# First group of a fused recommender tower in two parts: 16 samples at a time through gather, store, reload, pair products and x1, and W1 split in four pieces

## The chip, the cores and the metric

The kernel runs on one core of one Trainium2 chip. The metric is the device time of one execution in microseconds, taken as the median of several runs. Engines are named as in the profile: PE (matrix multiply), PEld (its weight loads), DVE (VectorE), ACT (ScalarE), POOL (GpSimd, which also issues the gathers and the folding transfers) and SP (SyncE, which issues the other transfers).

## The reference

There are 512 samples. For each, 39 rows of 16 numbers are gathered from 39 tables. Three interaction layers follow, each a sum over pairs of a raw field j and a field k of the layer before; then the three layers' sums over the 16 numbers and 16 dense features pass through a small three-layer network.

```
e  = stack([tbl_f[ids[:, f]] for f in 0..38])            # 512 x 39 x 16
x1 = einsum('hjk,bjd,bkd->bhd', W0, e, e)  + b0          # 128 fields
x2 = einsum('hjk,bjd,bkd->bhd', W1, e, x1) + b1
x3 = einsum('hjk,bjd,bkd->bhd', W2, e, x2) + b2
z  = concat([x1.sum(d), x2.sum(d), x3.sum(d)]);  h = concat([z, dense_ctx])
y  = relu(relu(h @ W_top1 + b) @ W_top2 + b) @ W_top3    # 512 x 1
```

## The kernel before

**Tiling.** A column is one (sample, d) pair, 8192 in all. A group is 512 columns (32 samples), a tile 128 columns; there are 16 groups of 4 tiles. Buffers exist twice, one half for even groups and one for odd.

**Getting a group's rows (x0).** POOL adds table starts to the ids (L317) and issues 10 indirect gathers for a group (L324), each for one row of 16 numbers on 125 partitions. SP stores them to a scratch tensor in device memory (L245) and loads them back turned (L255), so that a field is a partition and the group's 512 columns lie along it, in copies one below the other (for groups 0 and 1 all four pieces from memory, later one from memory and three copied inside SBUF, L259). SP then makes the shifted copies from which pairs are formed: three transfers for the first factor (L268), one for each second factor (L273). Second factors 1 to 6 share three slots, so number 4, 5 and 6 wait until earlier pairs are formed. After its last shifted copy SP goes on to the store and the reload of the next group.

**x1.** DVE forms seven blocks of pairs (L653, 117 x 512 each, two buffers); PE multiplies each by W0 folded over symmetric pairs (L394, full fp32) into one bank; ACT adds the bias (L542) and rounds the result to a high part x1_hi (L551); DVE computes the rest x1_lo (L660).

**x2.** For each of a group's 4 tiles PE does 10 chunks of 4 fields j (the last has 3): x1_hi times W1_hi, x1_hi times W1_lo, x1_lo times W1_hi (L426 to L428), into five banks in rotation. ACT takes six chunks of a tile and multiplies each unit by the column's x0 value (L567); DVE takes the other four and adds onto ACT's (L671). POOL then issues a transfer that adds one half of the tile's products onto the other half (L346, 'fold'), and DVE adds up the rest (L703, four steps), the first of which waits for that transfer. The x2 of tile t is summed beside tile t + 2. A third product with a diagonal matrix that POOL builds (L334) gathers sums over d for layer 3 (L411 on PE, L556 on ACT), one tile later still. Layer 3 and the small network come after the last group.

**Order of the work.** Every engine's program is written out by hand. Inside a group the position p = 10 * tile + chunk (0 to 39) is the clock: `FORM_AT` says after which chunk DVE forms a block of pairs for the next group (6, 10, ... 30), `PAIR_AT` where PE multiplies it (11, 15, ... 35), position 8 is where PE transposes the next group's x0 (L402), ACT takes bias and x1_hi of the next group behind chunk 35 (`BIAS_AT`), DVE x1_lo at 36, and the sums of DVE (`SUM_AT`) come at chunks 1, 3, 5 and 7 of a tile. So the first sum of tile 0 is at position 21.

**The start.** SP loads ids, table starts, the two halves of W0, W1 (2.4 MB), then eleven small constants. POOL issues the 10 gathers of group 0, the 10 of group 1 and, once the constants are there, 9 of the 10 of group 2 (`GATHERS_EARLY`), one behind the other (L350 to L358); only then comes its work of group 0, where in its second tile it issues the fold of tile 0:

```
if fold_before:
    scaled(t - 1)
diagonal(t, s, first)
if fold_before:
    fold((s - 1) % TILES_PER_GROUP)
```

ACT rounds W1 whole (L592), DVE takes the rest whole (L728), PE runs matmuls with no use (`warm_up`, L448) around the first transposes and the seven pair products, and starts group 0 when x1_lo is there.

Of the kernel before, what the change touches and what calls it, by code (L numbers as in the profile page):

```python
# [25 lines left out]
P = 128  # L26
COLS = 512
# [39 lines left out]
PIECES = [(0, 3), (3, 4)]  # L67
TOP1, TOP2 = 512, 256
# [5 lines left out]
AHEAD = 2  # L74
GATHERS_EARLY = 9
# [3 lines left out]
BIAS_AT = 5  # L79
# [6 lines left out]
def tower_program(nc, ids, starts, table, dense_t, pair_a, pair_b, w1, w2, b0, b1, b2,  # L86
# [6 lines left out]
    with ctx:  # L93
# [12 lines left out]
        idx = sb("idx", [ROW_PARTS, 2, GATHERS], i32)  # L106
        emb = sb("emb", [ROW_PARTS, 2, GATHERS * D])
# [56 lines left out]
        g_psum = small_bank[:, 0:TB * J1].rearrange("p (j b) -> p j b", b=TB)  # L164
        x0t_psum = x0t_bank[:, 0:TILES_PER_GROUP * F].rearrange("p (s f) -> p s f", f=F)


        ids_loaded = sem("ids_loaded")
        w_loaded = sem("w_loaded")
# [43 lines left out]

        def scaled_before(t, c):
# [9 lines left out]
        def _(sp):  # L224
            sp.dma_start(ids_all[:, :], ids).then_inc(ids_loaded, 16)
            sp.dma_start(table_at[:, :], starts).then_inc(ids_loaded, 16)
            sp.dma_start(pair_a_raw, pair_a).then_inc(w_loaded, 16)
            sp.dma_start(pair_b_raw, pair_b).then_inc(w_loaded, 16)
            sp.dma_start(w1_raw, w1).then_inc(w_loaded, 16)
            for slot in range(TILES_PER_GROUP):  # L230
# [11 lines left out]
            def store_rows(g, half):  # L242

                sp.wait_ge(gathered[half], (g + 2 - half) * (8 * GATHERS))
                sp.dma_start(emb_dram[bass.ds(g * ROW_PARTS, ROW_PARTS), :], emb[:, half, :]).then_inc(emb_stored, 16)  # L245

            def load_x0(g, half, at_once):


                sp.wait_ge(emb_stored, (g + 1) * 16)  # L250
# [10 lines left out]
            def factors(g, half):  # L261

                if not (isinstance(g, int) and g == 0):
                    sp.wait_ge(pair_ready, g * BLOCKS)
# [17 lines left out]
            x0_of(0, 0, at_once=True)  # L282
            factors(0, 0)
# [25 lines left out]
        def _(pool):  # L309
            pool.memset(x0t[:, :, :], 1.0).then_inc(ones_set, 1)  # L310
            pool.wait_ge(ids_loaded, 16 * 2)

            def index(g, half):

                if not (isinstance(g, int) and g < 2):
                    pool.wait_ge(gathered[half], (g - half) * (8 * GATHERS))
                pool.tensor_tensor(idx[:, half, :], ids_all[:, bass.ds(g * GATHERS, GATHERS)], table_at[:, :],  # L317
                                   ALU.add).then_inc(index_ready, 1)
                pool.wait_ge(index_ready, g + 1)
                if not (isinstance(g, int) and g < 2):  # L320
                    pool.wait_ge(emb_stored, (g - 1) * 16)
# [66 lines left out]
        def _(pe):  # L388
            def pair_product(g, b):

                pe.wait_ge(pair_ready, g * BLOCKS + (b + 1))
                if b == 0 and not (isinstance(g, int) and g == 0):
# [4 lines left out]
            def transpose_x0(half, first):  # L397

                if first:
                    pe.wait_ge(x0_loaded, 16 * X0_LOADS)  # L400
                for s in range(TILES_PER_GROUP):
                    mm = pe.transpose(x0t_psum[:, s, :], rep[0:F, half, s * P:(s + 1) * P], ident[:, :])  # L402
                mm.then_inc(x0t_mm, 1)
# [26 lines left out]
            def group(g, half, first=False, last=False):  # L430
                for s in range(TILES_PER_GROUP):
                    t = g * TILES_PER_GROUP + s
                    pe.wait_ge(x1_lo_ready, g * len(PIECES) + (1 if s < 3 else 2))
                    for c in range(CHUNKS):
                        p = s * CHUNKS + c
                        t_chunk(t, s, c, first and s == 0, g + 1 if p == X0T_AT and not last else None)
                        if c == G_AT and not (first and s <= BEHIND):
                            g_product(t - BEHIND - 1, (s - BEHIND - 1) % TILES_PER_GROUP)
                        if not last:
                            if p == X0T_AT:  # L440
                                transpose_x0(1 - half, False)
                            if p in PAIR_AT:
                                pair_product(g + 1, PAIR_AT.index(p))
# [10 lines left out]
            transpose_x0(0, True)  # L454
            warm_up(WARM_UP[1])
            for b in range(BLOCKS):
                pair_product(0, b)
# [367 lines left out]
```

## Time and profile before

| | us |
|---|---|
| median of 3 runs | 673.19 (672.38 to 675.87) |
| the profiled execution's own time | 672.67 |
| its span, first to last instruction | 670.6 |
| first matmul of group 0 | 44.37 |
| first matmul of group 1 | 79.71 |

```profile
POOL 6878766575656565755666675656575221121000
PEclk9799999999999999999999999999999999999999
```

The lines cut the span into 40 equal slices of 16.8 us; a digit is the busy share in tenths (for PEclk the share of full speed that TensorE's clock was granted). Line numbers L.. are those of the kernel before. Gathers and folding transfers stand with POOL as the time that it takes to issue them; they land later.

### The profile page before, as it was taken

The page shows a single profiled execution, that of the slowest core. Times are in us where ns is not written, and L with a number is a line of the kernel's source. Part 1 is how long each engine was busy: PE and PEld are TensorE (multiplying, and loading weights), DVE is VectorE, ACT ScalarE, POOL GpSimd, SP SyncE. Part 2 cuts the span into 40 slices and gives each one's busy share as a digit, 9 for nine tenths or more (in the row PEclk, how much of TensorE's full clock was granted, in tenths as well). Part 3 has the DMA queues.
Part 4 walks back from the last instruction along what each step waited for, and adds up shares of the span by engine and source line. Part 5 has one row for each costly group of instructions (what it writes and reads, how often), then busy time and mean ns, then how long its engine had stood idle before and what let it go on. Part 6 is the DMA issues. An engine that isn't in the chain of part 4 may idle for free.

```text
span 670.6 us, 11899 instructions
## 1 busy us (share of the span) xinstructions
PE 641.9 (96%) x2516; PEld 461.4 (69%) x2516; DVE 521.2 (78%) x1478; ACT 488.3 (73%) x1692; POOL 361.1 (54%) x308
## 2 busy tenths in 40 slices
PE   0689999999999999999999999999999999999998
PEld 0246777777777777777777777777777777785483
DVE  0346888878888888888888878888888888897590
ACT  1137877778787868787877878787868787897293
POOL 6878766575656565755666675656575221121000
PEclk9799999999999999999999999999999999999999
DMA  6457687767676777667667767676777657567100
GB/s 225 60 92 168 112 183 133 173 131 162 124 160 128 159 150 163 142 134 155 139 144 134 167 130 161 124 160 129 160 150 162 142 102 178 126 122 215 31 1 0
DMA packets 61944, 91.05 MB, mean 136 GB/s; under 512 B 34599, under 2 KB 38548, under 8 KB 61671
## 3 DMA queue, kind: packets, MB, share of 16 engines
q0 software_dynamic: 14192, 51.02, 42.0%
q1 hardware_dynamic: 47734, 39.85, 21.2%
q8 instruction: 6, 0.10, 0.1%
q14 instruction: 12, 0.09, 0.0%
HBM read 10.59 MB, written 1.28 MB: 18 GB/s over the span
## 4 chain that ended last, share of the span: by engine, by line
PE 91%; POOL 3%; DMA 3%; issue 2%; SPq 1%; ACT 0%; DVE 0%; ACTq 0%; POOLq 0%
PE t_bank L426 22%; PE t_bank L427 21%; PE t_bank L428 21%; PE x_bank L394 14%; PE small_bank L411 5%; POOL emb L324 3%; PE t_bank L491 1%; PE t_bank L471 1%; PE t_bank L502 1%; PE t_bank L503 1%; PE t_bank L514 1%; PE t_bank L505 1%; DMA emb<-in_table,idx 1%; PE x0t_bank L402 1%; DMA emb_scratch<-emb 1%
## 5 line engine op out<-in xcount | busy, mean ns | idle before, releaser
L567 ACT ACTIVATE prod<-t_bank,x0t 128x128 f32<-128x128 f32 x1472 | 417.5, 377 | 114.6 <-PE t_bank L428 109.3
L671 DVE SCALAR_TENSOR_TENSOR prod<-t_bank,x0t,prod 128x128 f32<-128x128 f32 x1024 | 287.9, 343 | 80.1 <-PE t_bank L428 75.8
L426 PE MATMUL t_bank<-w_hi,x_hi 128*128 128x512 f32 (+1 forms) x640 | 307.5, 480 | 0.6 <-DVE x_lo L660 0.3
L427 PE MATMUL t_bank<-w_lo,x_hi 128*128 128x512 f32 (+1 forms) x640 | 247.8, 387 | 0.0
L428 PE MATMUL t_bank<-w_hi,x_lo 128*128 128x512 f32 (+1 forms) x640 | 247.0, 386 | 0.0
L324 POOL DMA_INDIRECT emb<-in_table,idx x160 | 211.8, 1324 | 48.5 <-issue 46.8
L334 POOL TENSOR_TENSOR diag<-x0t,mask 128x320 f32<-128x320 f32 x64 | 87.8, 1372 | 195.4 <-DVE prod L671 97.7
L426 PEld LDWEIGHTS t_bank<-w_hi,x_hi 128*128 128x128 f32 x640 | 120.2, 188 | 54.7 <-issue 29.7
L427 PEld LDWEIGHTS t_bank<-w_lo,x_hi 128*128 128x128 f32 x640 | 120.5, 188 | 47.1 <-issue 25.3
L428 PEld LDWEIGHTS t_bank<-w_hi,x_lo 128*128 128x128 f32 x640 | 120.1, 188 | 24.2
L703 DVE TENSOR_TENSOR prod<-prod 128x768 f32<-128x768 f32 (+2 forms) x192 | 117.4, 611 | 6.0 <-DMA prod<-prod 5.7
L394 PE MATMUL x_bank<-pairs,w_pair 117*128 117x512 f32 x224 | 114.6, 594 | 2.7 <-DVE pairs L653 1.9
L653 DVE TENSOR_TENSOR pairs<-shared 117x512 f32<-117x512 f32 x96 | 65.5, 682 | 6.8 <-DMA shared<-rep 6.8
L346 POOL DMA_DIRECT2D prod<-prod x63 | 60.5, 961 | 0.0
L394 PEld LDWEIGHTS x_bank<-pairs,w_pair 117*128 117x128 f32 x224 | 41.8, 190 | 15.6 <-DVE pairs L653 6.3
L411 PE MATMUL small_bank<-diag,x 128*128 128x320 f32 x128 | 45.0, 433 | 0.0
L556 ACT ACTIVATE G<-small_bank 128x320 f32 (+1 forms) x64 | 29.1, 454 | 4.8 <-PE small_bank L411 4.8
L448 PE MATMUL t_bank<-w_pair 117*128 117x512 f32 x20 | 13.2, 816 | 16.3 <-DVE w_pair L726 16.3
L411 PEld LDWEIGHTS small_bank<-diag,x 128*128 128x128 f32 x128 | 23.9, 188 | 6.8 <-issue 0.8
L534 ACT ACTIVATE x0t<-x0t_bank 128x39 f32<-128x39 f32 x64 | 13.8, 221 | 10.7 <-PE x0t_bank L402 9.2
L542 ACT ACTIVATE x<-x_bank,bias 128x512 f32<-128x512 f32 x16 | 11.4, 715 | 13.2 <-PE x_bank L394 13.2
L625 ACT ACTIVATE w_hi<-G 128x512 fp32r<-128x512 f32 x20 | 12.6, 632 | 11.5 <-PE t_bank L505 10.5
(73 smaller groups left out, 242.8 us busy)
## 6 DMA issues: line engine op xcount, KB each, us to landing
prod<-prod POOLq DMA_DIRECT2D x63, 768.0 KB, 7.1
shared<-rep SPq DMA_DIRECT2D x96, 234.0 KB
shared<-rep SPq DMA_DIRECT2D x48, 78.0 KB
emb<-in_table,idx POOLq DMA_INDIRECT x160
G<-in_w SPq DMA_DIRECT2D x1, 2496.0 KB
rep<-rep SPq DMA_DIRECT2D x28, 78.0 KB
rep<-emb_scratch SPq DMA_DIRECT2D x20, 78.0 KB
prod<-in_w SPq DMA_DIRECT2D x1, 1536.0 KB, 7.1
```

Source lines behind the costliest of these rows:

```text
L324: pool.indirect_dma_start(out=emb[:, half, i * D:(i + 1) * D], out_offset=None, in_=table, in_offset=bass.IndirectOffsetOnAxis(ap=idx[:, h ...
L334: pool.tensor_tensor(diag[:, slot, :, :], x0t[:, slot, :].unsqueeze(2).to_broadcast([P, J1, TB]), mask[:, :].unsqueeze(1).to_broadcast([P, ...
L346: pool.dma_start(prod[:, slot, 0:HALF, :].rearrange("p j h -> p (j h)"), prod[:, slot, HALF:, :].rearrange("p j h -> p (j h)"), accum_op=A ...
L394: pe.matmul(x1_bank[:, :], w_pair[:, b * H:(b + 1) * H], pairs[:, b % 2, :], start=b == 0, stop=b == BLOCKS - 1).then_inc(pair_mm, 1)
L411: pe.matmul(small_bank[:, 0:TB * J1], x2[:, slot % 2, :], diag[:, slot, :, :].rearrange("p j b -> p (j b)"), start=True, stop=True).then_i ...
L426: pe.matmul(acc, hi, w1_hi[:, cols], start=True, stop=False)
L427: pe.matmul(acc, hi, w1_lo[:, cols], start=False, stop=False)
L428: pe.matmul(acc, lo, w1_hi[:, cols], start=False, stop=True).then_inc(t_mm, 1)
L567: last = act.activation(prod[:, s, SLOT[c] + u, :], t_bank[c % T_BANKS][:, u * H:(u + 1) * H], ACT.Copy, scale=x0t[:, s, j:j + 1])
L653: dve.tensor_tensor(pairs[:, b % 2, :], first, rep[0:PAIRS, half, :] if b == 0 else second[:, k, :], ALU.mult).then_inc(pair_ready, 1)
L671: last = dve.scalar_tensor_tensor(unit, t_bank[c % T_BANKS][:, u * H:(u + 1) * H], x0t[:, s, j:j + 1], unit, ALU.mult, ALU.add)
L703: dve.tensor_tensor(out, left, right, ALU.add).then_inc(summed, 1)
```

## The change

Group 0 is handled as two parts of 16 samples (256 columns, 2 tiles). A part has a gather of its own: two samples' halves folded on 126 (124) partitions, so 5 gathers a part in place of 10 for the group. It has its own ids (four small loads a part: part 0's ahead of the weights, part 1's and then the whole ids behind W1), its own store (2 transfers), reload (4), shifted copies (3 + 6) and semaphores. The six second factors of a part lie in space of `prod` that is free then, so they need no slot. Part 0's x1 is made before group 0 starts, in a bank of its own; part 1's is made inside group 0, with pairs at positions 7 to 13, products at 10 to 16, x1_hi ahead of chunk 17 and x1_lo at 18. What group 0 does for group 1 moves back: x0 transposes from position 8 to 22, pairs from 6, 10, ... 30 to 24, 26, ... 36, products from 11, 15, ... 35 to 26, 28, ... 38, bias and x1_hi from behind 35 to behind 39, x1_lo from 36 to 39. The later groups are as before. W1 is rounded and its rest taken in pieces of 10, 10, 10 and 9 fields. POOL's order behind the parts (group 1's gathers, 9 of group 2, then group 0's diagonals and folds) stays.

```diff
+PARTS = 2
+W1_PIECES = [(0, 10), (10, 20), (20, 30), (30, F)]
+PART_X0T_AT = 8
+PART_FORM_AT = [7 + b for b in range(BLOCKS)]
+PART_PAIR_AT = [10 + b for b in range(BLOCKS)]
+PART_X1_AT = (1, 7)
+PART_LO_AT = 18
+FIRST_Z0_AT = 21
+FIRST_X0T_AT = 22
+FIRST_FORM_AT = [24 + 2 * b for b in range(BLOCKS)]
+FIRST_PAIR_AT = [p + 2 for p in FIRST_FORM_AT]
+FIRST_X1_AT = (3, 9)
+FIRST_LO_AT = 39
 # SP
-            sp.dma_start(ids_all[:, :], ids).then_inc(ids_loaded, 16)
-            sp.dma_start(table_at[:, :], starts).then_inc(ids_loaded, 16)
+            load_part_ids(0)
             sp.dma_start(pair_a_raw, pair_a).then_inc(w_loaded, 16)
             sp.dma_start(pair_b_raw, pair_b).then_inc(w_loaded, 16)
             sp.dma_start(w1_raw, w1).then_inc(w_loaded, 16)
+            load_part_ids(1)
+            sp.dma_start(ids_all[:, :], ids).then_inc(ids_loaded, 16)
+            sp.dma_start(table_at[:, :], starts).then_inc(ids_loaded, 16)
...
-            x0_of(0, 0, at_once=True)
-            factors(0, 0)
+            for part in range(PARTS):
+                x0_of_part(part)
+                factors_of_part(part)
 # POOL
+            def gather_part(part):
+                n = FOLDS * PART_SIZE[part]
+                pool.wait_ge(part_ids_loaded[part], 16 * PART_IDS_LOADS)
+                pool.tensor_tensor(part_idx[0:n, part, :], part_ids[0:n, part, :], part_at[0:n, part, :],
+                                   ALU.add).then_inc(part_index_ready, 1)
+                pool.wait_ge(part_index_ready, part + 1)
+                for c in range(PART_GATHERS):
+                    pool.indirect_dma_start(
...
-            for g in range(AHEAD):
-                index(g, g)
-                for i in range(GATHERS):
-                    gather(i, g)
+            for part in range(PARTS):
+                gather_part(part)
+            pool.wait_ge(ids_loaded, 16 * 2)
+            index(1, 1)
+            for i in range(GATHERS):
+                gather(i, 1)
             pool.wait_ge(small_loaded, 16 * SMALL_LOADS)
 
             index(AHEAD, 0)
 # PE, in group 0
+                        if first and p in PART_PAIR_AT:
+                            last_part_pair_product(PART_PAIR_AT.index(p))
 # ACT
-            act.activation(w1_hi[:, :], w1_raw, ACT.Copy).then_inc(w_split_hi, 1)
+            for a, b in W1_PIECES:
+                act.activation(w1_hi[:, a * H:b * H], w1_raw[:, a * H:b * H], ACT.Copy).then_inc(w_split_hi, 1)
```

## Rows read from the trace of the kernel before

**Rows 1.** the page, engine shares and the chain that ended last

```profile
PE 641.9 (96%) x2516; PEld 461.4 (69%) x2516; DVE 521.2 (78%) x1478; ACT 488.3 (73%) x1692; POOL 361.1 (54%) x308
...
PE 91%; POOL 3%; DMA 3%; issue 2%; SPq 1%; ACT 0%; DVE 0%; ACTq 0%; POOLq 0%
```

**Rows 2.** busy time of engines by stretch; PEclk is the granted clock

```profile
21.80:27.90 6.10, 0.63 (x2) 0.01 (x1) 3.15 (x2) 0.00 (x0) 5.49 (x3) 0.87 0.51 51
28.40:32.10 3.70, 3.70 (x7) 1.57 (x6) 0.00 (x0) 0.49 (x4) 3.03 (x3) 0.50 0.42 95
...
79.70:115.60 35.90, 35.90 (x147) 26.73 (x146) 30.10 (x91) 28.36 (x105) 23.00 (x19) 1.00 0.72 148
115.60:151.60 36.00, 35.98 (x147) 26.74 (x146) 30.30 (x92) 28.47 (x105) 21.57 (x19) 1.00 0.71 149
```

**Rows 3.** timeline of the start: start us, us, engine, line, operation

```profile
3.99 1.43 POOL L324 DMA_INDIRECT emb<-in_table,idx  x1 [0.33 <-POOL idx L317]
...
11.75 0.43 SPq L238 DMA_DIRECT2D w<-in_top  x1
...
15.13 4.36 ACT L592 ACTIVATE w_hi<-G 128x4992 fp32r<-128x4992 f32 x1 [13.09 <-DMA G<-in_w]
...
19.52 5.36 DVE L728 TENSOR_TENSOR w_lo<-G,w_hi 128x4992 fp32r<-128x4992 f32 x1 [3.30 <-ACT w_hi L592]
...
19.64 6.35 POOL L324 DMA_INDIRECT emb<-in_table,idx  x1 [0.30 <-POOL idx L317]
...
20.65 0.30 SPq L245 DMA_DIRECT2D emb_scratch<-emb  x1
...
40.15 0.22 POOL L317 TENSOR_TENSOR idx<-ids_all,table_at 125x10 int32<-125x10 int32 x1
...
42.39 0.69 ACT L542 ACTIVATE x<-x_bank,bias 128x512 f32<-128x512 f32 x1 [13.24 <-PE x_bank L394]
...
44.37 0.47 PE L426 MATMUL t_bank<-w_hi,x_hi 128*128 128x512 f32 x1 [0.30 <-DVE x_lo L660]
```

**Rows 4.** groups by line, POOL, 4 to 19 us

```profile
L324 POOL DMA_INDIRECT emb<-in_table,idx x10 | 12.4, 1236 | 3.1 <-issue 2.7 <-POOL idx L317 0.3
```

**Rows 5.** timeline of POOL, group 0: the fold of tile 0

```profile
57.58 0.99 POOL L346 DMA_DIRECT2D prod<-prod  x1
```

**Rows 6.** timeline of DVE in groups 0 and 1

```profile
62.04 0.68 DVE L653 TENSOR_TENSOR pairs<-shared 117x512 f32<-117x512 f32 x1
64.48 0.96 DVE L703 TENSOR_TENSOR prod<-prod 128x768 f32<-128x768 f32 x1 [1.77 <-DMA prod<-prod]
65.36 1.12 DVE L671 SCALAR_TENSOR_TENSOR prod<-t_bank,x0t,prod 128x128 f32<-128x128 f32 x4
...
87.66 0.69 DVE L653 TENSOR_TENSOR pairs<-shared,rep 117x512 f32<-117x512 f32 x1 [0.58 <-DMA shared<-rep]
```

**Rows 7.** issues by line: KB each, median us to landing

```profile
shared<-in_top SPq DMA_DIRECT2D x1, 768.0 KB, 5.1
...
shared<-in_top SPq DMA_DIRECT2D x1, 32.0 KB, 5.0
```

**Rows 8.** the chain in order of time: one pair product

```profile
65.08 0.86 PE x_bank L394 x2
```

**Rows 9.** timeline of PE around the start of group 1

```profile
79.71 0.51 PE L426 MATMUL t_bank<-w_hi,x_hi 128*128 128x512 f32 x1
...
89.03 1.02 PE L394 MATMUL x_bank<-pairs,w_pair 117*128 117x512 f32 x2
```

**Rows 10.** timeline of SP, groups 2 and 3

```profile
63.85 0.32 SPq L245 DMA_DIRECT2D emb_scratch<-emb  x1
...
81.06 2.37 SPq L268 DMA_DIRECT2D shared<-rep  x3
```

**Rows 11.** timeline of SP, one group later

```profile
99.61 0.32 SPq L245 DMA_DIRECT2D emb_scratch<-emb  x1
...
114.37 2.38 SPq L268 DMA_DIRECT2D shared<-rep  x3
```

More of the change, by code:

```diff
@@ L224, in _, with load_part_ids @@
         def _(sp):
-            sp.dma_start(ids_all[:, :], ids).then_inc(ids_loaded, 16)
-            sp.dma_start(table_at[:, :], starts).then_inc(ids_loaded, 16)
+            def load_part_ids(part):
+                begin, n = PART_BEGIN[part], PART_SIZE[part]
+                for to, src in ((part_ids, ids), (part_at, starts)):
+                    for fold in range(FOLDS):
+                        sp.dma_start(to[fold * n:(fold + 1) * n, part, :],
+                                     src[begin:begin + n, fold:fold + PART_IDS]).then_inc(part_ids_loaded[part], 16)
+            load_part_ids(0)
             sp.dma_start(pair_a_raw, pair_a).then_inc(w_loaded, 16)
@@ L391, in pair_product @@
                 pe.wait_ge(pair_ready, g * BLOCKS + (b + 1))
-                if b == 0 and not (isinstance(g, int) and g == 0):
+                if b == 0:
                     pe.wait_ge(x1_ready, g)
@@ L395, in pair_product, with part_pair_product, last_part_pair_product, transpose_x0 @@
                           start=b == 0, stop=b == BLOCKS - 1).then_inc(pair_mm, 1)
[L397 to L401, printed above, removed]
+            def part_pair_product(b):
+                pe.wait_ge(early_pair_ready, b + 1)
+                pe.matmul(part_x1, w_pair[:, b * H:(b + 1) * H], pairs[:, b % 2, part_cols(0)],
+                          start=b == 0, stop=b == BLOCKS - 1).then_inc(early_pair_mm, 1)
+            def last_part_pair_product(b):
+                pe.wait_ge(pair_ready, b + 1)
+                pe.matmul(x1_bank[:, part_cols(1)], w_pair[:, b * H:(b + 1) * H], pairs[:, b % 2, part_cols(1)],
+                          start=b == 0, stop=b == BLOCKS - 1).then_inc(pair_mm, 1)
+            def transpose_x0(half, tiles=range(TILES_PER_GROUP), done=x0t_mm):
+                for s in tiles:
                     mm = pe.transpose(x0t_psum[:, s, :], rep[0:F, half, s * P:(s + 1) * P], ident[:, :])
-                mm.then_inc(x0t_mm, 1)
+                mm.then_inc(done, 1)
             def g_product(t, slot):
@@ L524, in _, with copy_x0t @@
         def _(act):
-            def copy_x0t(g, s, first):
+            def copy_x0t(g, s, first=False):
                 t = g * TILES_PER_GROUP + s
-                act.wait_ge(x0t_mm, g + 1)
+                if first and s < PART_TILES:
+                    act.wait_ge(early_x0t_mm, 1)
+                else:
+                    act.wait_ge(x0t_mm, g + 1)
                 if not first:
@@ L571, in group @@
             def group(g, first=False, last=False):
+                x1_at = FIRST_X1_AT if first else X1_AT
                 for s in range(TILES_PER_GROUP):
```

221 lines of the change are left out of this document (169 added, 52 removed).

## The prediction

> **What bounds the kernel now.** I read the page first: PE is busy 96% of the span and holds 91% of the chain that ended last [rows 1]. The windows by stretch say whether that is real: in groups 1 and 2 PE is busy 35.90 of 35.90 and 35.98 of 36.00 us at a granted clock of 1.00, while DVE has 30.1 and ACT 28.4 [rows 2]. So a group costs 36 us of PE, nothing later gives back what a group loses, and what remains outside is the start: group 0's first matmul is at 44.37 us [rows 3], group 1's at 79.71 [rows 9]. The question is by how much the change moves group 1's start, and what group 1 finds late.
>
> The timeline of the start shows POOL as the engine in front: 29 gathers one behind the other, 10 of group 0, 10 of group 1 and 9 of group 2, each 1.24 us and some 0.3 apart [rows 4], so 1.51 us each. One is much longer: the gather that starts at 19.64, just behind the start of DVE's W1 rest (19.52, 5.36 us), takes 6.35 us and ends 1.1 us behind DVE's end [rows 3]. Only when all 29 are out does POOL reach group 0, and its fold of tile 0 is issued at 57.58 [rows 5]. DVE's first sum of tile 0 (position 21) starts at 64.48, having waited 1.77 us for that transfer: 6.9 us after the issue [rows 5, 6]. Today PE starts so late that this hardly shows. A group 0 that starts earlier runs into it.
>
> **Part by part.**
>
> *The start itself.* Part 0 needs 5 gathers. Its ids are four loads in place of two, so the first gather goes from 3.99 to some 4.7 and the five are in at 14. SP, though, has six more loads to issue before it comes to the store: its list ended at 11.75 + 0.43 [rows 3], 16 loads in 11.4 us, 0.7 each (small ones less); 6 more give 14.5 to 16.5, I take 15.5, where the store was at 20.65. From that store to the first matmul were 23.7 us; half-width pairs, no slot waits and half-width x1 take some 5 of it (estimate; 1 to 9). Group 0 then starts at about 34 (30 to 39), 10 us earlier. The W1 pieces end near 22.5 instead of 24.9; nothing waits for them, as x1 is later. They cost nothing: the ACT and DVE time is hidden beside the gathers.
>
> *What POOL does to it.* Gathers are 29 as before. Two things differ. Part 1's ids are issued behind W1, which landed at 15.13 [rows 3] and is pushed to about 15.9 by the loads ahead. Do small loads wait for a large one ahead of them on the same queue? In the end of the trace a 32 KB load issued right behind a 768 KB one took 5.0 us, the large one 5.1 [rows 7]: yes. So part 1's first gather is at about 16.9, where POOL could have gone on at 12.4: 4.5 us idle. (The Trainium skill, DMA: Bandwidth & Descriptors, section Queues, rings and completion order, says that SP's transfers use one ring per DMA engine and are taken from it in ring order; the trace agrees as far as the 5.0 us go. Without that rule the stall would be nothing.) And DVE's four W1 pieces, about 17.0 to 22.5, lie right beside part 1's five gathers. The one long gather stretched by 5.1 us; in pieces the same 5.4 us can hold up between 1 and 4.5 us, I take 2.2. (The Trainium skill, GPSIMD Engine Reference, section 8, Key points, has GpSimd sharing its SBUF interfaces with VectorE, with contention where a VectorE instruction has two SBUF inputs, which the W1 rest has; the row agrees. It gives no duration.) Part 1 ends at 16.9 + 5 x 1.51 + 2.2 = 26.6, the index work is 0.55, group 1's ten gathers with the first a little longer and 0.3 of holds 15.6: group 2's index at 42.7 where it was at 40.15 [rows 3]. From there POOL's order is unchanged, 17.4 us to the fold and 6.9 to its landing. So DVE's sum of tile 0 can start at F = 67.0, not at 64.48: +2.5. Bounds: no wait for ids and no holds give -4.0 (20 gathers at 1.51 and three index steps from 4.7), all holds +4.7.
>
> *Part 1 inside group 0.* Its rows come at about 28, store 30 to 35, reload to 40, copies to 50; its pairs (position 7 on) wait, its products are seven of half width, 0.43 us each (0.86 for the full pair of matmuls [rows 8]), 3 us of PE. PE passes position 20 near 57. Chunks may run five banks ahead, so PE stands at position 26 by 61. All this lies before 67.0, so it costs nothing now; without that cover it would be 3 us of PE and some 6 of waits.
>
> *From F to group 1.* Before, 79.71 - 64.48 = 15.2 us, with four products of the next group left. Now all seven are left, and the first cannot start before DVE has done, behind the wait, two sums (0.96 [rows 6] and about 0.5), chunks 22 and 24 (1.12 each [rows 6]) and the first block of pairs (0.68): 4.1 us with their overlaps. Then 7 products x 0.86 = 6.0 and positions 27 to 39. A position is (36.0 - 6.0) / 40 = 0.75 us of PE, its small products shared in [rows 2], so 13 x 0.75 = 9.8. Form and product stand two positions apart, where it was five; pairs take 0.68 and a chunk 1.12 of DVE in 2.4 us of PE, so DVE just keeps up, no charge. At the boundary bias and x1_hi now come behind ACT's last chunk: 1.1 us for its three scalings, and 1.98 from bias to first matmul, as in the start (42.39 to 44.37 [rows 3]). Sum 4.1 + 6.0 + 9.8 + 3.1 = 23.0, 7.8 more than before. Below, PE's head start of three positions could be better used (+5); above, late forms (+9).
>
> *The clock.* PE idles from about 61 to 71. After an idle stretch of 6 us (21.8 to 27.9, PE busy 0.63) the granted clock was 0.50, that is 1.2 GHz of 2.4, over the next 3.7 us [rows 2]. Half of that is lost where PE binds: +1.5 (0 to 2.2).
>
> *What group 1 finds late.* SP stores group 2 only after its last shifted copy of group 1, which waits for the fourth block of pairs. Before: that block at 62.04, store at 63.85 [rows 6, 10], group 2's first pairs at 87.66, after a wait of 0.58, so 23.8 us with nothing to spare. Now the fourth block is at position 30: F + 4.2 + two products + four positions + its own 0.6 and the slow clock, F + 11 = 78.0; store 79.8; first pairs at 103.6, or 101.2 at the pace of a group later, where the store to the first-factor copy took 14.8 us (99.61 to 114.37) and not 17.2 [rows 10, 11]. The product follows 1.4 us later [rows 6, 9], 102.6 to 105.0. PE would want it 9.3 us after group 1's start [rows 9], 91.5 + 9.3 = 100.8. So PE waits 1.8 to 4.2 us more; I take 2, since the new stretch has fewer folds beside it. From group 2 on the periods are as before: the same block is at 18 again, with 22 positions to the next form.
>
> *Sum.* +2.5 + 7.8 + 1.5 + 2.0 = +13.8 on the profiled execution's own 672.67 (span 670.6 and 2.1 around it): 686.5. The median of the runs is 0.5 above that execution, well inside the uncertainty. The ten microseconds won at the start all become waiting in front of tile 0's sum.
>
> **Rivals.** (1) *The fold binds, but little is added behind it.* The clock is not charged because DVE sets the pace there, group 2's rows come at the quick pace, PE's head start is used: +1 + 5 + 0 + 0 to 2, about 679.5. For it: terms of one stretch overlap, as DVE and PE are near equal there. Against: the first form stands behind DVE's wait, and the boundary chain is serial. (2) *POOL is early, no slower than before.* If part 1's ids land early and the pieces leave gaps between them, the fold is issued 4.0 us earlier (53.6), and beside a quieter queue it could land in the shortest time that any fold of this trace took, 3.9 us in place of 6.9: F = 57.5. With +7.8 group 1 starts at 80.5, less 1 to 3 where PE has stood only briefly and kept its clock and head start: 78 to 80.5, and the time is 671 to 673.5. It decides from F below 56.7 (79.71 - 23.0). Against it are the 5.0 us of the small load and 29 gathers at 1.51, which no piece shortens. (3) *The gain passes.* If the sum of tile 0 did not hold the others up (chunks 22 to 26 going on from the banks while the fold lands, and the fold out by 50), the kernel would keep 10.4 of the start, less 3.0 of products and 3.1 at the boundary: 668. Against: DVE's list is in order, the sum stands ahead of chunk 22, and POOL's 29 gathers alone fill 4.7 to 50. (4) *The copies for part 1 are still later than the fold:* it needs 17 us more than I have for them; then 690 and up.
>
> **How the numbers follow.** Forecast 686.5: 0.55 (its own range 681 to 692); rival 1: 0.24; rival 2: 0.08; rival 3: 0.08; rival 4: 0.05. A change under 0.5% (3.4 us) can hardly be told from none with these runs. Faster 0.10 (rival 3 and a piece of 2), same 0.08, slower 0.82. The range 674 to 692 takes in rival 1 and the bounds of the holds.
>
> **What would show it.** In the changed trace: first matmul of group 0 at 30 to 39; POOL idle from about 12.4 to 16.5 before part 1's index; the W1 rest in four pieces with stretched gathers beside it; fold of tile 0 issued near 60; DVE's first 128x768 sum with a wait of 5 to 12 us on that transfer, near 67; PE idle before that, then a granted clock near 0.5; about 3 us between the last chunk of group 0 and group 1's first matmul, which is at 88 to 93; a wait of PE for group 2's first pairs; and periods of 36 us from then on. I am wrong if the first sum starts before 57, if group 1's first matmul is before 79, or if later groups take less than 35.9.

## The result, and the profile after

| | before | after |
|---|---|---|
| median of the runs, us | 673.3 (4 runs) | 699.45 (4 runs, 695.48 to 702.86) |
| ratio, 95% interval | | 1.037 [1.0322, 1.0417] |
| own time of the profiled execution, us | 672.67 | 695.48 |
| span, us | 670.6 | 693.5 |
| first matmul of group 0, us | 44.37 | 39.95 |
| DVE's first sum of tile 0, us | 64.48 | 64.88 |
| first matmul of group 1, us | 79.71 | 90.28 |
| what is lost behind that, us | 0 | 12.3 |

The change makes the kernel 3.7% slower, more than the 2% of the forecast and outside its range. Of the 22.9 us by which the span grew (22.8 by own time), 10.6 are there when group 1 starts (90.28 - 79.71); the other 12.3 come later, where nothing had been forecast. The profiled execution is the shortest of the four runs after, so the median is 4.0 us above the sums made on it.

The page first. Its instruction queue (q14) carried 12 packets before and carries 40 now, and of the chain that ended last 75% is PE, 8% DVE and 6% 'issue', where PE had 91% and 'issue' 2% [rows 1]. Before, then after:

```profile
q14 instruction: 12, 0.09, 0.0%
```

```profile
PE 650.8 (94%) x2530; PEld 464.9 (67%) x2530; DVE 521.9 (75%) x1489; ACT 490.5 (71%) x1697; POOL 346.5 (50%) x309
...
q14 instruction: 40, 0.33, 0.1%
...
PE 75%; DVE 8%; issue 6%; DMA 6%; SPq 3%; ACT 1%; DVEq 1%; POOL 0%; POOLq 0%; ACTq 0%
```

The windows by stretch come next, 36 us each from group 1's start (five of them; columns as in [rows 2]: length, sum busy of PE, PEld, DVE, ACT, POOL, then clock, DMA share, GB/s).

```profile
...
162.00:198.00 36.00, 35.46 (x143) 25.77 (x142) 29.39 (x88) 27.59 (x101) 21.02 (x19) 1.00 0.70 144
198.00:234.00 36.00, 35.98 (x148) 26.78 (x147) 30.28 (x92) 28.47 (x104) 23.13 (x20) 1.00 0.70 147
234.00:270.00 36.00, 34.61 (x141) 25.18 (x140) 29.52 (x88) 26.86 (x99) 19.84 (x19) 1.00 0.64 135
270.00:306.00 36.00, 35.98 (x149) 26.79 (x147) 30.30 (x91) 28.47 (x105) 21.60 (x20) 1.00 0.71 148
306.00:342.00 36.00, 34.53 (x140) 25.10 (x139) 28.84 (x86) 27.10 (x98) 19.79 (x18) 1.00 0.65 136
```

Every second group is whole (35.98 busy of 36, as all groups were before [rows 2]), and the ones between have 35.46, 34.61 and 34.53. The stretches slip as the kernel falls behind, so they show that there is a loss, not its exact size. The distance from each group's first matmul to the next group's gives the size: groups 3, 5, 7, 9, 11 and 13 take 37.1, 37.9, 38.0, 38.0, 38.9 and 37.8 us, all others from group 1 on 36.0 or less (before, every group takes 35.9 to 36.0). That is 11.7 us in six groups; the other 0.6 lies behind the start of the last group. The loss recurs once per pass of the loops: a pass holds two groups, and these six are the ones that begin a further pass. DVE's timeline at one of these places shows what it is (start us, us, engine, line, operation, idle before and what ended it):

```profile
234.97 0.29 DVE L878 TENSOR_TENSOR x<-prod 128x128 f32<-128x128 f32 x1
235.18 1.12 DVE L846 SCALAR_TENSOR_TENSOR prod<-t_bank,x0t,prod 128x128 f32<-128x128 f32 x4
240.06 0.96 DVE L878 TENSOR_TENSOR prod<-prod 128x768 f32<-128x768 f32 x1 [3.76 <-issue]
```

DVE ends its last chunk of group 4 at 236.3 and does nothing until 240.06, and the profile names no releaser: 'issue'. The sum at 240.06 is DVE's first work of group 5, the first that the third pass of the loop does behind the branch. Grouped over the loop:

```profile
L878 DVE TENSOR_TENSOR prod<-prod 128x768 f32<-128x768 f32 x171 | 106.0, 620 | 29.7 <-issue 22.9 <-DMA prod<-prod 6.7
```

22.9 us of 'issue' in 6 places, 3.8 each; PE loses 11.7 of them, about half. In the trace of before no sum waits for 'issue' in the loop (115 to 640 us); all that they wait for there is (us in total, times, longest):

```profile
DVE prod L703 <- DMA prod<-prod: 4.0, 5, 2.4
```

The start, SP first, then POOL, then DVE's first sum of tile 0:

```profile
4.46 6.50 SPq L278 DMA_DIRECT2D part_at<-in_starts  x2
11.01 2.35 SPq L286 DMA_DIRECT2D ids_all<-in_ids  x1
...
18.81 1.88 SPq L345 DMA_DIRECT2D emb_scratch<-part_emb  x2
24.55 1.83 SPq L351 DMA_DIRECT2D rep<-emb_scratch  x4
```

```profile
14.97 0.21 POOL L402 TENSOR_TENSOR part_idx<-part_ids,part_at 124x9 int32<-124x9 int32 x1 [4.42 <-DMA part_at<-in_starts]
15.49 2.50 POOL L406 DMA_INDIRECT part_emb<-in_table,part_idx  x1 [0.31 <-POOL part_idx L402]
18.30 2.48 POOL L406 DMA_INDIRECT part_emb<-in_table,part_idx  x1 [0.31 <-issue]
21.08 1.28 POOL L406 DMA_INDIRECT part_emb<-in_table,part_idx  x1 [0.30 <-issue]
...
41.13 0.22 POOL L415 TENSOR_TENSOR idx<-ids_all,table_at 125x10 int32<-125x10 int32 x1
...
58.38 1.00 POOL L444 DMA_DIRECT2D prod<-prod  x1
```

```profile
64.88 0.96 DVE L878 TENSOR_TENSOR prod<-prod 128x768 f32<-128x768 f32 x1 [5.40 <-DMA prod<-prod]
```

And the stretches of PE around the end of group 0 (columns as above):

```profile
60.00:64.40 4.40, 4.37 (x21) 3.04 (x19) 0.00 (x0) 3.72 (x15) 3.76 (x4) 1.00 0.99 184
64.40:69.00 4.60, 0.00 (x0) 0.00 (x0) 4.12 (x12) 0.47 (x2) 3.77 (x4) 0.92 0.93 222
69.00:72.00 3.00, 2.97 (x5) 1.75 (x6) 2.01 (x7) 0.00 (x0) 1.21 (x1) 0.50 0.96 193
72.00:75.00 3.00, 3.00 (x7) 1.75 (x6) 1.30 (x5) 1.14 (x4) 0.00 (x0) 0.50 0.47 123
...
77.00:87.30 10.30, 10.30 (x38) 6.77 (x36) 7.17 (x22) 5.98 (x24) 5.26 (x5) 1.00 0.71 139
87.30:90.30 3.00, 0.20 (x2) 0.03 (x1) 0.74 (x2) 1.99 (x5) 1.56 (x2) 1.00 0.21 57
```

PE does nothing from 64.4 to 69.0 and works at 0.50 of its clock (1.2 GHz) for the 6 us behind; then it stands idle from 87.3 to 90.3. The chain of waits shows the last stretch as single steps, one behind the other: ACT's last scalings, bias, x1_hi, DVE's x1_lo, PE.

```profile
58.38 6.48 DMA prod<-prod
...
87.78 0.62 ACT prod L706 x2
88.40 0.59 ACT x L681
89.01 0.53 ACT x_hi L690
89.56 0.57 DVE x_lo L835
90.28 0.49 PE t_bank L535
```

### The profile page after: what moved, and what is told of

Same layout as the page of the kernel before. It is cut to its first block, busy times and chain, and to the rows that moved or that the text cites. A ratio compares the mean times of both kernels' runs of the same rounds, so it can differ in the third digit from the quotient of the medians.

```text
span 693.5 us, 11966 instructions
## 1 busy us (share of the span) xinstructions
PE 650.8 (94%) x2530; PEld 464.9 (67%) x2530; DVE 521.9 (75%) x1489; ACT 490.5 (71%) x1697; POOL 346.5 (50%) x309
## 3 DMA queue, kind: packets, MB, share of 16 engines
HBM read 10.61 MB, written 1.28 MB: 17 GB/s over the span
## 4 chain that ended last, share of the span: by engine, by line
PE 75%; DVE 8%; issue 6%; DMA 6%; SPq 3%; ACT 1%; DVEq 1%; POOL 0%; POOLq 0%; ACTq 0%
PE t_bank L535 17%; PE t_bank L536 16%; PE t_bank L537 16%; PE x_bank L494 13%; DVE prod L846 5%; DMA prod<-prod 4%; PE small_bank L520 4%; DVE prod L878 2%; SPq L278 1%; PE t_bank L611 1%; PE t_bank L623 1%; PE t_bank L625 1%; PE t_bank L622 1%; PE t_bank L634 1%; DMA emb_scratch<-part_emb 1%
## 5 line engine op out<-in xcount | busy, mean ns | idle before, releaser
L535 PE MATMUL t_bank<-w_hi,x_hi 128*128 128x512 f32 (+1 forms) x640 | 311.2, 486 | 12.3 <-DVE prod L846 7.8
L422 POOL DMA_INDIRECT emb<-in_table,idx x150 | 190.5, 1270 | 45.4 <-issue 44.5
L432 POOL TENSOR_TENSOR diag<-x0t,mask 128x320 f32<-128x320 f32 x64 | 80.5, 1258 | 228.2 <-ACT prod L706 101.7
L878 DVE TENSOR_TENSOR prod<-prod 128x768 f32<-128x768 f32 (+2 forms) x192 | 118.6, 617 | 35.2 <-issue 22.9
L494 PE MATMUL x_bank<-pairs,w_pair 117*128 117x512 f32 x210 | 109.2, 601 | 4.7 <-DVE pairs L828 4.7
L828 DVE TENSOR_TENSOR pairs<-shared 117x512 f32<-117x512 f32 x90 | 61.3, 681 | 1.6 <-DMA shared<-rep 1.6
L494 PEld LDWEIGHTS x_bank<-pairs,w_pair 117*128 117x128 f32 x210 | 40.0, 192 | 12.8 <-DVE pairs L828 5.1
L567 PE MATMUL t_bank<-w_pair 117*128 117x512 f32 x20 | 14.6, 891 | 15.2 <-DVE w_pair L907 15.2
L775 ACT ACTIVATE w_hi<-G 128x512 fp32r<-128x512 f32 x20 | 12.6, 632 | 11.5 <-PE t_bank L625 10.5
L944 DVE TENSOR_TENSOR w_lo<-G,w_hi 128x512 fp32r<-128x512 f32 x20 | 13.7, 692 | 8.2 <-ACT w_hi L775 8.1
```

What stands on the lines that cost most here:

```text
L422: pool.indirect_dma_start(out=emb[:, half, i * D:(i + 1) * D], out_offset=None, in_=table, in_offset=bass.IndirectOffsetOnAxis(ap=idx[:, h ...
L432: pool.tensor_tensor(diag[:, slot, :, :], x0t[:, slot, :].unsqueeze(2).to_broadcast([P, J1, TB]), mask[:, :].unsqueeze(1).to_broadcast([P, ...
L494: pe.matmul(x1_bank[:, :], w_pair[:, b * H:(b + 1) * H], pairs[:, b % 2, :], start=b == 0, stop=b == BLOCKS - 1).then_inc(pair_mm, 1)
L535: pe.matmul(acc, hi, w1_hi[:, cols], start=True, stop=False)
L828: dve.tensor_tensor(pairs[:, b % 2, :], first, rep[0:PAIRS, half, :] if b == 0 else second[:, k, :], ALU.mult).then_inc(pair_ready, 1)
L878: dve.tensor_tensor(out, left, right, ALU.add).then_inc(summed, 1)
```

## The experiments

The theory after this reading had two halves: (a) in the start, what the forecast says, that POOL's order and the crowded end of group 0 eat the gain; (b) in the loop, that DVE fetches its program anew in every pass, because its loop now begins 16 instructions later. Counted in the built programs, DVE's loop is 308 instructions in both and begins at number 126 before and 142 after. The rival to (b) was that some transfer is late in every second group. Each time below is the median of its runs; the ratio is to runs of the kernel before on the same chip. The runs stem from several chips, on which the kernel before had medians of 672.9 to 675.7, so kernels of different chips are compared by ratio. Places within a kernel (a first matmul, a wait) are those of its one profiled execution. How far such places scatter can be seen from e2 and e10 below, whose start is that of the kernel before but for idle instructions: group 0's first matmul came at 46.04 and 45.65 where it was 44.37, group 1's at 80.62 and 80.79 where it was 79.71.

**e1: the changed kernel, DVE's loop moved 60 instructions on** (142 to 202), by waits that are already met, where DVE idles:

```diff
 # DVE, ahead of its first work
+            for _ in range(120):
+                dve.wait_ge(part_ids_loaded[0], 16 * PART_IDS_LOADS)
```

> The changed kernel with 120 waits that are already met (60 instructions) on DVE ahead of its first work, where it idles 14 us; nothing else. Theory (loop place): the changed kernel's two-group loop on DVE, 308 instructions long as before, begins 16 instructions later in DVE's program, no longer fits in what DVE holds of its program, and is fetched anew in each of its 7 passes; that is the 1.5 to 2.5 us that PE loses in every second group (12 of the 22.8 us). 60 instructions further on it fits again: some 12 us faster than the changed kernel (about 683 to 687), the waits of DVE's first sum for 'issue' gone, instruction-queue packets back from 40 to near 12. Rival (the gathers or transfers are late in every second group): the time stays at 695 to 700 and the waits stay.

Measured: 685.62 us, ratio 1.0156 [1.0098, 1.0214], where the changed kernel had 1.037 [1.0322, 1.0417]. Instruction queue and windows of the middle, which are whole again:

```profile
q14 instruction: 11, 0.08, 0.0%
```

```profile
223.70:259.70 36.00, 35.97 (x148) 26.76 (x147) 30.18 (x90) 28.37 (x103) 23.15 (x20) 1.00 0.70 146
259.70:295.70 36.00, 35.99 (x148) 26.78 (x147) 30.27 (x90) 28.36 (x103) 23.06 (x20) 1.00 0.70 146
...
```

So 60 instructions that do nothing make the kernel 2.1% faster, and the place of DVE's loop is the cause. Only DVE's loop was moved; those of the other engines begin where they do in the changed kernel. That the stall is a fetch is read from the packets and from the waits that name no releaser.

This profiled execution (687.17) is not free of loss behind group 1's start either. Group 1 starts 9.2 us later than in the kernel before, and 5.4 us more are lost after it: 1.6 in group 1, whose first 3 us (90 to 93) have a granted clock of 0.55 after PE's wait at the boundary; 2.5 in group 2, where DVE waits for group 3's first-factor copies; 1.3 behind the start of the last group.

```profile
88.92 0.49 PE L535 MATMUL t_bank<-w_hi,x_hi 128*128 128x512 f32 x1 [2.80 <-DVE x_lo L835]
```

```profile
137.49 0.69 DVE L828 TENSOR_TENSOR pairs<-shared,rep 117x512 f32<-117x512 f32 x1 [3.71 <-DMA shared<-rep]
```

The 1.6 us of group 1 recur in e5, e6, e7 and e9, the wait for copies does not.

**e2 and e10: the kernel before, DVE's loop moved 16 and 48 instructions on** (126 to 142 and 174), 32 and 96 met waits on `ids_loaded` in the same place.

> The kernel before with 32 met waits (16 instructions) on DVE ahead of its first work, so that its loop begins at the same instruction as the changed kernel's. Loop place: 10 to 14 us slower than before (683 to 687), PE windows of every second group at 33.5 to 35 us busy of 36, some 40 instruction-queue packets. Rival (something in the two parts disturbs the later groups): as before, 673.

Measured: 682.5 us, ratio 1.0121 [1.0078, 1.0165], 41 packets. A kernel that computes exactly what the one before does, with 16 idle instructions, loses 8 us, a little less than the 10 to 14 expected; by its trace groups 3, 5, ... 13 take 1.2 to 1.7 us more than the others, 8.9 in all.

> The kernel before with 96 met waits (48 instructions) on DVE ahead of its first work: DVE's loop begins at instruction 174 of its program, between the places that were slow (142) and fast again (202 to 204) and the fast one of before (126). If what counts is how many fixed blocks of the program the loop lies across (blocks of 256 by the Trainium skill, Runtime: NRT & Kernel Launch, section Instruction fetch mechanics), the edges seen so far put 174 still across three: as e2, 681 to 684, 38 to 42 packets of the instruction queue. Rival (16 instructions met one bad place only, for example one branch at an unlucky address): as before, 673, about 10 to 12 packets.

Measured: 679.8 us, ratio 1.0094 [1.0068, 1.012], 41 packets: slow, as the theory said, if by less (681 to 684 expected). DVE's waits in the loop, e2 and then e10 (who waited for whom: us in total, times, longest):

```profile
DVE prod L703 <- issue: 19.5, 6, 3.6
```

```profile
DVE prod L703 <- issue: 12.2, 6, 2.4
```

Both lose it in the same 6 passes, 3.3 and 2.0 us each. Places 126 and 129 (e11, e12) are fast, 142 and 174 slow, 202 and 204 fast. (The Trainium skill, Runtime: NRT & Kernel Launch, section Instruction fetch mechanics, says that an engine other than PE holds two blocks of 256 instructions, and that a taken branch whose target is in neither stalls until its block is fetched. An estimate from the figures in that section of the Trainium skill: a loop of 308 fits if it begins at most 204 behind the edge of a block, and the places seen agree if 63 to 75 instructions stand ahead of the built program, which no run here shows. The packets, 28 more over 7 passes of the loop, are 4 for each pass.)

**e3: the changed kernel, POOL's order.**

```diff
+FIRST_EARLY = 5
+FIRST_REST = [range(0), range(5, 10), range(0), range(0)]
+FIRST_NEXT = [range(0), range(0), range(0, 5), range(5, 9)]
...
-            for i in range(GATHERS_EARLY):
+            for i in range(FIRST_EARLY):
                 gather(i, 0)
...
+                    if first:
+                        for i in FIRST_REST[s]:
+                            gather(i, half)
+                        for i in FIRST_NEXT[s]:
+                            gather(i, 1 - half)
+                        continue
...
```

> The changed kernel with POOL's order in the start changed: 5 of group 2's gathers ahead of group 0's work in place of 9, the other 5 behind the fold of tile 0, and 5 and 4 of group 3's in tiles 2 and 3. Theory (POOL's order holds the fold of tile 0 up): the fold is issued at about 52 instead of 58.4, DVE's first sum starts at about 59 without a wait of 5.4, PE keeps its clock, and group 1's first matmul comes 7 to 10 us earlier than 90.3. Rival (the late pairs and the serial end of group 0 set it): under 3 us. The later groups stay as in the changed kernel, so the whole is 688 to 692 against 695 to 700.

Measured: 700.57 us, ratio 1.0383 [1.0335, 1.043]: nothing gained, where 688 to 692 were expected. The fold was issued at 55.67 (not 52; POOL had to wait for tile 0 to be scaled) and the first sum's wait fell from 5.4 to 1.5 us. But:

```profile
54.88 5.18 SPq L316 DMA_DIRECT2D rep<-emb_scratch  x4
64.02 2.41 SPq L328 DMA_DIRECT2D shared<-rep  x3
```

```profile
64.04 0.50 PE L544 MATMUL t_bank<-w_hi,x_hi 128*128 128x512 f32 x1 [2.21 <-DMA rep<-emb_scratch]
```

```profile
62.46 0.96 DVE L887 TENSOR_TENSOR prod<-prod 128x768 f32<-128x768 f32 x1 [1.54 <-DMA prod<-prod]
...
72.43 0.69 DVE L837 TENSOR_TENSOR pairs<-shared,rep 117x512 f32<-117x512 f32 x1 [2.84 <-DMA shared<-rep]
```

Group 1's reload, issued at 54.88, now runs beside the folding transfer and is not there before 64.0 (5.1 us from first issue to the shifted copies in the changed kernel, 9.1 here); PE waits 2.2 us for it, DVE 2.8 us for the first-factor copies, and group 1 starts at 91.44. My theory that POOL's order was the bound is true only up to the next one, less than 5 us behind, and removing the first pushed the second back.

**e4, e11, e12: parts of the change in the kernel before, without cutting the group.** e4 gives group 0's second factors 4 to 6 a place in `prod`, e12 splits W1 in four, e11 does both.

```diff
                 for b in range(1, BLOCKS):
+                    if isinstance(g, int) and g == 0 and b > SECOND_SLOTS:
+                        sp.dma_start(late_at(b), rep[b:b + PAIRS, half, :]).then_inc(late_second[b - 1 - SECOND_SLOTS], 16)
+                        continue
                     if b > SECOND_SLOTS:
                         sp.wait_ge(pair_ready, g * BLOCKS + (b + 1 - SECOND_SLOTS))
...
```

> The kernel before with one part of the change alone: in group 0 the second factors 4 to 6 go to free space of prod instead of waiting for a slot. Theory: the last pairs of group 0 are formed at about 37.5 to 38.5 instead of 40.48, the first matmul of group 0 is at 41.5 to 42.5 instead of 44.37, and since nothing of group 0 is held up by a fold at that shift (DVE waited 1.8 us with no loss of PE), the kernel is 1.5 to 3 us faster, 670.5 to 672. Rival (the fold of tile 0 at 64.5 takes the gain): 673, with a longer wait of the first sum.

Measured: e4 673.53 us over 10 runs, ratio 0.9977 [0.9949, 1.0004]. Group 0's first matmul came at 43.62 (41.5 to 42.5 expected), group 1's at 78.81, 0.8 and 0.9 us earlier than in the kernel before. DVE still waits for the last copies, and its last three blocks of pairs come at 37.56, 38.61 and 39.73, where 37.5 to 38.5 was expected for the last. The interval takes in 1, and 0.9 us is within the scatter of such places, so no gain is shown. (Its profiled execution is the slowest of its ten, 678.79, with its losses behind group 1's start.)

> The kernel before with W1 split in four pieces alone. Theory: nothing waits for the rest of W1 (x1 is later), so the same time within 1 us; the gather at 19.64 that took 6.35 us becomes two or three of 1.5 to 2.7 and group 1's rows are there 1 to 3 us earlier, hidden. Rival: those earlier rows shorten DVE's wait of 2.6 us for group 1's first pairs and give up to 1 us.

Measured: e12 674.84 us over 12 runs, ratio 1.0025 [1.0003, 1.0048]: a little slower, just clear of 1. Neither the theory (within 1 us) nor the rival (up to 1 us faster) fits. POOL and SP:

```profile
18.23 2.50 POOL L325 DMA_INDIRECT emb<-in_table,idx  x1 [0.30 <-issue]
```

```profile
22.28 0.30 SPq L246 DMA_DIRECT2D emb_scratch<-emb  x1
25.00 2.96 SPq L256 DMA_DIRECT2D rep<-emb_scratch  x4
```

Begun early, DVE's four pieces (15.4 to 20.9) fall on group 0's own last gathers (18.23: 2.50 us instead of 1.21), and group 1's gathers, no longer held, run beside group 0's store and reload: store at 22.28 where it was 20.65, reload 5.6 us long instead of 4.9, first matmul 47.44 instead of 44.37. Group 1 starts 1.9 us later. Of this, 1.3 to 1.7 and 0.9 to 1.1 us are no more than e2 and e10 show without any split. That in the kernel before the long W1 operation keeps POOL quiet just when group 0 needs the DMA engines is therefore the likely reading of these rows, not a shown cause.

> The kernel before with two parts of the change that do not cut the group: second factors 4 to 6 of group 0 in prod (as e4) and W1 split in four pieces. DVE's loop begins 3 instructions later than before; by e2 it went wrong at 16. Expected as e4, 0.5 to 2.5 us faster than before (671 to 673), the W1 pieces adding nothing but a shorter stretched gather; if 3 instructions are enough to push the loop out, 9 us slower.

Measured: e11 673.62 us over 12 runs, ratio 1.0 [0.9975, 1.0025], where 671 to 673 was expected. As far as these intervals can tell the two cancel; 3 instructions further on, the loop still fits (11 packets).

**e5, e6, e9: what else is in the end of group 0,** all on e1 (with its 60 idle instructions; e1 has a ratio of 1.0156 and group 1's start at 88.92). e5 moves group 0's work for group 1 forward, e6 lets DVE fold tile 0, e9 does both.

```diff
-FIRST_FORM_AT = [24 + 2 * b for b in range(BLOCKS)]
+FIRST_FORM_AT = [22 + 2 * b for b in range(BLOCKS)]
-FIRST_X1_AT = (3, 9)
-FIRST_LO_AT = 39
+FIRST_X1_AT = (3, 7)
+FIRST_LO_AT = 38
```

> The padded changed kernel (e1) with group 0's work for group 1 moved forward by two positions: forms at 22 to 34, products 24 to 36, bias and x1_hi ahead of ACT's chunk 38 (behind 37), x1_lo at 38. Theory (the end of group 0 is serial: 2.8 to 3 us between its last matmul and group 1's first): the gap shrinks to under 1 us and group 1 starts 2 to 3 us earlier than 88.9, the whole 2 to 3 us under e1. Rival (rows or the fold set it): the gap shrinks and the same time is waited at the first product; no gain.

Measured: 682.57 us, ratio 1.0129 [1.0083, 1.0176]. Group 1 starts at 86.22, 2.7 us earlier than in e1, as expected. Its wait at the boundary is 1.84 us instead of 2.80 (under 1 expected), and its first product waited 1.85 us instead of 4.22.

```diff
+                elif isinstance(t, int) and t == 0:
+                    dve.wait_ge(act_scaled, NA)
+                    dve.wait_ge(dve_scaled, ND)
+                    dve.tensor_tensor(prod[:, slot, 0:HALF, :], prod[:, slot, 0:HALF, :], prod[:, slot, HALF:, :],
+                                      ALU.add).then_inc(first_folded, 1)
...
```

> The padded changed kernel (e1) with the fold of tile 0 done by DVE itself (one more 128x1408 addition, some 1.5 us) and no folding transfer for that tile. Theory (the fold of tile 0 is what PE waits for): the 5.4 us wait of DVE goes, the first product of group 1 comes at 64 to 66 instead of 69.2, PE's clock stays at full, group 1 starts at 82 to 85 instead of 88.9 and the whole is 4 to 6 us faster than e1. Rival (group 1's rows are just behind the fold): DVE waits for the first-factor copies instead, product at 67 to 69, 0 to 2 us faster.

Measured: 681.15 us, ratio 1.0124 [1.0065, 1.0183]. The first product comes at 66.23, group 1 at 86.36. Between theory and rival: DVE's own addition in place of the folding transfer was worth 2.6 us of group 1's start, and PE's clock stayed at 1.00 up to there.

> e5 and e6 together (padded changed kernel; group 0's work for group 1 two positions earlier; tile 0 folded by DVE), the weights again from SP. If the two gains are of different stretches, group 1 starts at 83 to 85 and the whole is 677 to 680, still slower than the kernel before (group 1 at 79.7), because part 1's seven products and the seven late ones are PE time. Rival (both touch the same bound, group 1's rows): as e5 or e6 alone, 681 to 682.5.

Measured: 679.9 us, ratio 1.0094 [1.0062, 1.0126]. PE around the start of group 1 in e5, e6 and e9:

```profile
67.32 1.13 PE L494 MATMUL x_bank<-pairs,w_pair 117*128 117x512 f32 x2 [1.85 <-DVE pairs L828]
...
86.22 0.49 PE L535 MATMUL t_bank<-w_hi,x_hi 128*128 128x512 f32 x1 [1.84 <-DVE x_lo L835]
```

```profile
66.23 1.12 PE L495 MATMUL x_bank<-pairs,w_pair 117*128 117x512 f32 x2 [1.34 <-DVE pairs L829]
...
86.36 0.49 PE L536 MATMUL t_bank<-w_hi,x_hi 128*128 128x512 f32 x1 [2.94 <-DVE x_lo L836]
```

```profile
83.75 0.49 PE L536 MATMUL t_bank<-w_hi,x_hi 128*128 128x512 f32 x1 [1.84 <-DVE x_lo L836]
```

By group 1's start the gains add (2.7 and 2.6 alone, 5.2 together), and it is still 4.0 us later than in the kernel before. In the whole time the ratios fall the same way, 1.0156, 1.0129, 1.0124, 1.0094, but these four intervals overlap: the times alone do not show a gain over e1.

**e7, e8: the weights out of SP's way.** e7 is e1 with the three weight loads issued by ACT and both parts' ids first on SP; e8 is e9 with that.

```diff
 # SP
             load_part_ids(0)
-            sp.dma_start(pair_a_raw, pair_a).then_inc(w_loaded, 16)
-            sp.dma_start(pair_b_raw, pair_b).then_inc(w_loaded, 16)
-            sp.dma_start(w1_raw, w1).then_inc(w_loaded, 16)
             load_part_ids(1)
 # ACT
+            act.dma_start(pair_a_raw, pair_a).then_inc(w_loaded, 16)
+            act.dma_start(pair_b_raw, pair_b).then_inc(w_loaded, 16)
+            act.dma_start(w1_raw, w1).then_inc(w_loaded, 16)
```

> The padded changed kernel (e1) with the three weight loads issued by ACT instead of SP, and both parts' ids first on SP. Theory (SP and part 1's ids stand behind the weights): POOL has no idle 4.4 us before part 1's index, SP's store of part 0 is issued at 12.5 to 14 instead of 19.5, group 0's first matmul is at 33 to 36 instead of 40.3, and the fold of tile 0 is issued 4 us earlier (about 54); the whole 3 to 5 us faster than e1. Rival (the start does not matter, what follows tile 0's sum does): first matmul early, time within 1.5 us of e1.

Measured: 690.95 us, ratio 1.0276 [1.021, 1.0341] against e1's 1.0156 [1.0098, 1.0214]: not the 3 to 5 us faster that were expected, and most likely slower than e1. Group 0's first matmul is at 42.58 (33 to 36 expected), group 1's at 95.02. POOL:

```profile
12.60 0.20 POOL L399 TENSOR_TENSOR part_idx<-part_ids,part_at 126x9 int32<-126x9 int32 x1 [11.61 <-DMA part_at<-in_starts]
```

The ids of part 0 had been there at 3.5. From ACT the weights (3.3 MB) start at the same moment as the ids, not 1.5 us behind them, and the ids land at 12.6, as late as W1 (ACT begins to round it at 12.72). Ids ahead of the weights on one queue were worth 9 us of POOL's time. The theory about SP's queue was right that it is crowded and wrong about the cure.

> e5, e6 and e7 in one kernel, to see whether the two parts can beat the kernel before at all. If the terms add: 685.6 less 3, 5 and 4 us, about 673 to 675, level with the kernel before; it would be ahead (under 671) only if group 1's rows come early enough as well. Rival: one bound remains (the seven late products of 0.86 us and part 1's 3 us of products are PE time whatever the order), 677 to 680.

Measured: 684.6 us, ratio 1.014 [1.0085, 1.0196], neither the 673 to 675 of the sum nor the rival's 677 to 680; with the late ids in it, it says nothing for the sum of the gains, which e9 gives.

## Why the prediction was wrong

**The step that failed** is the last sentence on what group 1 finds late: "From group 2 on the periods are as before". They are not: 12.3 us are lost there, 11.7 of them in the six groups that begin a further pass, by DVE's loop being fetched again in each pass. e1 takes this loss out of the changed kernel (1.037 to 1.0156) and e2 puts most of it into the old one (1.0121). No part of the change's intent is in it, only its 16 more instructions ahead of the loop. I had written that the later groups are unchanged because their code is; the place of the code was not looked at, and the one row of before that could have warned, 12 packets on the instruction queue over a loop of 7 passes, only says that it fitted, not how nearly. Without this the measured kernel is e1, 685.6 or 1.0156, against a forecast of 686.5 or 1.021.

**That agreement is partly luck.** e1's profiled execution has 9.2 us at group 1's start where 11.8 was forecast (2.5 + 7.8 + 1.5), and 5.4 us behind it where 2.0 was. The terms of the changed kernel's profiled execution show the same:

| step | forecast | measured |
|---|---|---|
| first matmul of group 0 | 34 | 39.95 |
| tile 0's first sum | +2.5 (67.0) | +0.4 (64.88) |
| from it to group 1's first matmul | 23.0 + 1.5 clock, +9.3 | 25.4, +10.2 |
| group 2's rows late | +2.0 | 0 |
| sum up to group 1's first matmul | +11.8 | +10.6 |
| sum with group 2's rows | +13.8 | +10.6 |
| later groups | 0 | +12.3 |

- *The start* was 6 us later than worked out and outside its bounds of 30 to 39. SP was stopped in the middle of its small loads, 6.50 and 2.35 us, behind the weights; I had taken the mean of 0.7 from a list in which the same stop is shorter. The store of part 0 was at 18.81, not 15.5, and it took 5.7 us from issue to the reload, where the group's took 2.2. That the time won at the start is waited away in front of tile 0's sum was right, so this did not matter to the end.
- *Part 1's ids behind W1*: right in kind; POOL idled 4.42 us (forecast 4.5). The W1 pieces held two gathers (2.50, 2.48), 2.4 us together (forecast 2.2). But a part's other gathers took 1.0 to 1.28 us, not 1.21 and more, and W1 landed at 14.0, not 15.9. That made the term 0.4: group 2's index at 41.13, the fold at 58.38, its landing 6.5 us later.
- *The wait for the fold* was there, 5.40 us on DVE and 4.7 on PE, and e6 shows what it was worth, 2.6 us of group 1's start; e3 shows that group 1's rows stood close behind it. I had not put a price on that second bound.
- *The end of group 0*: the two-position distance and the serial end cost what was forecast, within 1 us; the serial end is 3.0 us in the window, and e5 shows that it can be shortened by about 1.
- *The clock*: forecast 1.5 us of loss. PE was busy for 5.97 of the 6 us behind 69.0 at a granted clock of 0.50, so at most 3 us of its work was lost there (an estimate; no run separates it). PE had idled 4.6 us before that, not ten. A second fall was not forecast at all: behind the boundary the clock was 1.00 in the changed kernel's trace but 0.55 in e1's, after 2.80 us of idling in both; e1, e5, e6, e7 and e9 lose 1.6 us by it in group 1. Why the same wait has both outcomes is open.
- *Group 2's rows* were in time: DVE's wait was 0.27 us where it was 0.58 [rows 6], since group 2's store was issued at 77.84 (79.8 forecast) and the copies came 20.1 us behind it (21.4 to 23.8 forecast). In e1 the same kind of wait came one group later and cost 2.5 us.
- *Rivals*: the first puts +6 at group 1's start; the measured +10.6 is nearer the forecast's +11.8, and the clock, which this rival left uncharged, did fall. What it had right is that group 2's rows came in time. Rival 2 rested on a misread row: the 3.9 us of landing belong to another transfer into the same tile (512 KB of top weights, near the end); the folds of the kernel before took 5.7 to 7.8 us where their landing is on record, which would have put its F at 59.3. Rivals 2 to 4 did not occur. None named the loop.

What stays open: e2 and e10 lose 8.2 and 6 us, the changed kernel 12 to 14 by the same stall; its passes wait 3.8 us each against 3.3 and 2.0. Why the stall has these lengths was not tried. The profiled execution after is the shortest of its four (695.48; the others 698.0 to 702.86), and what the longer ones lose beyond it has no trace.

## What to carry to other kernels

A gain in the start is only worth what the next consumer can take: list the engines' in-order queues up to the first place where old and new meet (here 29 gathers ahead of a fold), and the second bound behind it, before pricing the start. A loop's cost can depend on where it begins in its engine's program; when an edit adds instructions ahead of a loop, compare the packets of the instruction queue and look for 'issue' waits that recur once per pass, and move the loop with idle instructions before judging the edit. No version here beats the kernel before clearly; e4, the shared slots' removal alone, is at 0.9977 with an interval that takes in 1. And compare a place in one trace with another only beyond what traces of the same code differ by, here 1 to 1.7 us in the start.

## What was unexpected of the hardware

- DVE's loop of 308 instructions ran without waits for 'issue' at its passes begun at 126, 129, 202 and 204, and DVE waited 2.0 to 3.8 us per pass begun at 142 and 174, with 40 or 41 packets on the instruction queue instead of 10 to 12.
- Small loads issued by SP at the moment when another engine issues 3.3 MB landed at 12.6 us; issued ahead of the same bytes on one queue they landed at 3.5.
- A long DVE operation on two SBUF tensors that holds a gather up may help: taken apart (e12) it let gathers loose beside the store and reload that were on the path, and group 0's first matmul came 3.1 us later, of which up to 1.7 is scatter; in the whole time 0.25% is left.
- TensorE's granted clock fell to 0.50 after 4.6 us without work and stayed there for about 6 us. After a wait of 2.80 us it fell in e1 (0.55 over the next 3 us) and did not in the changed kernel (1.00).
